# Cross attention with the probabilities turned on VectorE and placed by DMAs, sums two steps behind, text keys and values in a stage of their own

## The chip, the cores and the metric

The kernel runs on one core of one Trainium2 chip. The metric is the time of one execution on the device in microseconds (us), the median of several runs. The core has a matrix engine (TensorE; PE in the profile, PEld its weight loads), VectorE (DVE), ScalarE (ACT), GpSimd (POOL), a queue processor that issues DMAs (SP) and 16 DMA engines. The matrix engine writes to PSUM, 8 banks of 128 partitions by 2 KB; all else lies in SBUF, 128 partitions.

## What is computed

Six layers work on an array x of 16 batches, 64 tokens, 256 features, each adding its result to x: a local attention, a self attention and a mixture of experts, then the cross attention that is changed here, a state-space scan and a second mixture of experts. The cross attention has 16 heads of 64 features. A batch's 64 queries look at 1601 context rows, in two softmaxes: 77 text rows and 1524 image rows, each with keys and values from weights of its own.

```python
ctx_txt, ctx_img = context[:, :77], context[:, 77:]
q = (x @ Wq).reshape(B, N, 16, 64)
out    = attend(q, heads(ctx_txt @ Wk),    heads(ctx_txt @ Wv))     # softmax(q k^T / 8) v
out_ip = attend(q, heads(ctx_img @ Wk_ip), heads(ctx_img @ Wv_ip))
return (out + out_ip) @ Wo + bo
```

## The kernel before

Each layer is one or more stages; a stage ends when all engines have left it. The stages that matter here: `positions_stage` (where the local attention looks), `near_attention` (the local attention's common case), and `cross_attention`.

`cross_attention` keeps the raw context rows instead of image keys and values. For a batch and a pair of heads, `key_side` (L2145) multiplies the pair's 128 queries (2 heads by 64 tokens) by the key weights, giving `a` (128 queries by 256 features, turned). `scores` (L2159 to L2161) multiplies `a` by the context `ct` in three banks of 508 columns. To keep float32 exactness at the matrix engine's fast rate each operand is split into a rounded part (`hi`) and the rest (`lo`), so a product is three: hi by hi, hi by lo, lo by hi. 

A step is one batch and one pair of heads: 8 pairs by 2 batches are the 16 steps (`STEPS`) of a tile, and 8 tiles make 128 steps. In step n, in program order, TensorE does: the text scores (L2151) once the exponentials of step n-1 are there; the 12 transposes of step n-1's image probabilities (`turn`, L2169, blocks of 127 columns, to PSUM); scores of step n; the transpose of the text probabilities (`turn_text`, L2176); of the sums of step n-2 (`turn_sums`, L2190); `key_side` of step n+1; `sums` of step n-1 (L2182: `pt_hi` by `cn` hi and lo side by side, 512 columns; L2183: `pt_lo` by `cn` hi, 256 columns; 12 times each); `value_side` of step n-2 (L2201, L2203). In 8 steps of a tile it also makes a piece of the next text keys or values in float32 (`text_keys`, L2127, 3 pieces a tile; `text_values`, L2136, 4 pieces a tile), in one step the next tile's queries (L2117), and in one the output projection (L2213).

VectorE takes the row maxima of the scores in PSUM (L2417, L2418), makes the bias (L2421), the rest parts `a_lo` and `pt_lo` (L2308, reading the product's PSUM bank and the `hi` part), the reciprocals (L2408), scales the text probabilities (L2410) and adds the two halves of the sums (L2432, L2435). ScalarE copies `hi` parts out of PSUM (L2302), takes the exponentials with their sums (L2365 image, L2368 text) and makes the plain copies (L2332). The scores have one buffer (`s_ps`), so the text scores of step n+1 wait for `exp_done` of step n. The other products go round a ring of 3 banks (`Ring`, `t_ps`).

SP loads the context of the next batch in 8 pieces (L1900 `ct`, L2032 `cn`), one staging buffer for all; GpSimd splits each piece into hi (L1907) and lo (L1909), after which SP may load the next. In `near_attention` SP first issues 32 small DMAs that bring the positions back from device memory (`load_positions`, L303), for which GpSimd's L603 waits.

Of the kernel before, what the change touches and what calls it, by code (L numbers as in the profile page):

```python
# [20 lines left out]
BANK = 512  # L21
# [32 lines left out]
IB, IBLK = 12, 127  # L54
SB, SBLK = 3, 508
assert IB * IBLK == IMG and SB * SBLK == IMG
# [392 lines left out]

def near_attention(nc, k, src, ctx):  # L450
# [299 lines left out]
def far_attention(nc, k, src):  # L750
# [3 lines left out]
    with ExitStack() as ctx:  # L754
# [39 lines left out]
        def _(sp):  # L794
            load_positions(sp, k)
# [1071 lines left out]
class Ring:  # L1867

    def __init__(self, i, uses_per_tile, splits_per_tile, at, splits):
        assert uses_per_tile % RING == 0
        self.i, self.each, self.split_each, self.at, self.splits = i, uses_per_tile // RING, splits_per_tile, at, splits

    def place(self, back=0):

        at = self.at - back
        return at % RING, self.i * self.each + (at // RING + 1)

    def next(self, split=False):
        got = self.place()
        self.at += 1
        self.splits += 1 if split else 0
        return got

    def split_count(self):
        return self.i * self.split_each + self.splits

# [27 lines left out]
class CrossFirst:  # L1918
# [3 lines left out]
    def __init__(self, nc, scope, src):  # L1922
        def sb(name, shape, dt=F32):
# [6 lines left out]
        self.wk_txt = sb("wk1_txt", [P, C, INNER])  # L1930
        self.text = sb("text1", [P, C, 2, TXT])
        self.staged = sb("staged", [P, CNB * D])
        self.ct = sb("ct0", [P, 2, C, IMG], F32R)
        self.wq_in, self.wk_in, self.text_in, self.piece_in, self.hi_done, self.ct_split, self.split_begun = (
            scope.enter_context(nc.semaphore(n))
            for n in ("wq1_in", "wk1_in", "text1_in", "piece_in", "ctx_hi_done", "ct_split", "ctx_split_begun"))

    def load_weights(self, sp):
        sp.dma_start(self.wq, self.src["wq1"]).then_inc(self.wq_in, 16)
        sp.dma_start(self.wk_txt[:], self.src["wk1_txt"]).then_inc(self.wk_in, 16)  # L1940
        sp.dma_start(self.text[:], self.src["ctx_txt"][0]).then_inc(self.text_in, 16)
# [3 lines left out]
def cross_attention(nc, k, src, first):  # L1945

    STEPS = 2 * PAIRS1
    K_USES, V_USES = 3, 2
    USES = STEPS * 7 + 4 + K_USES + 2 * V_USES  # L1950
    SPLITS = STEPS * 4
    SCALE = HD1 ** -0.5
    with ExitStack() as ctx:
# [9 lines left out]
        staged, wk, wk_txt, text, wq = first.staged, first.wk, first.wk_txt, first.text, first.wq  # L1963
        wo = first.w_shared[:].rearrange("p (h d) -> p h d", h=PAIRS1)
        wv = sb("wv1", [P, 2, C, INNER])
# [7 lines left out]
        prob = sb("prob1", [P, M])  # L1973
        pt_hi, pt_lo = sb("pt_hi", [P, IB, P], F32R), sb("pt_lo", [P, IB, P], F32R)
        pt_txt = [sb(f"pt_txt{s}", [P, P]) for s in range(2)]
        top = [sb(f"top1{s}", [P, 2]) for s in range(2)]
        bias = [sb(f"bias1{s}", [P, 2]) for s in range(2)]
        total = [sb(f"total1{s}", [P, 2]) for s in range(2)]
        inv = [sb(f"inv1{s}", [P, 2]) for s in range(2)]
        o, o_part = sb("o1", [P, D]), sb("o1_part", [P, D])  # L1980
# [6 lines left out]
        text_in, text_used = first.text_in, sem("text1_used")  # L1987
        queried, projected, bo_added = sem("queried"), sem("projected"), sem("bo1_added")
        piece_in, hi_done, ct_split, cn_split = first.piece_in, first.hi_done, first.ct_split, sem("cn_split")
        scored, topped, bias_done, exp_done = sem("scored1"), sem("topped1"), sem("bias1_done"), sem("exp1_done")  # L1990
        t_done = [sem(f"t1_done{j}") for j in range(RING)]
        t_kept = [sem(f"t1_kept{j}") for j in range(RING)]
        hi_kept, txt_normed = sem("hi_kept"), sem("txt_normed")
        summed, inv_done, part_kept, sums_kept = sem("summed1"), sem("inv1_done"), sem("part1_kept"), sem("sums1_kept")
        q_zeroed = sem("q_zeroed")
        block = ctx.enter_context(nc.Block())

        def tiles(eng, body):

            start = 2 + K_USES + 1  # L2000
            body(0, Ring(0, USES, SPLITS, start, 1), True, False)
# [970 lines left out]
```

## Time and profile before

| | us |
|---|---|
| median of 3 runs | 2601.33 (2599.84 to 2604.13) |
| the profiled execution | 2598.55 |
| its span, first to last instruction | 2595.7 |
| cross attention on TensorE, 551.3 to 2168.4 | 1617.1 |

The profile describes one execution. Its page gives busy times by engine and groups of instructions; behind it stand the timeline (instructions in order of time, runs of the same merged, with the idle time ahead and what ended it), the waits (who waited for whom) and stretches (busy time within given bounds, with the clock granted to TensorE, 1.00 being full). A matmul's duration in a timeline runs to a modelled end and overlaps the next, so what one costs is the distance between starts. The page's slices show the granted clock of TensorE at nine tenths or more through the cross attention.

### The profile page before, as it was taken

What the parts mean: (1) busy time and instruction counts of PE and PEld (TensorE: products, weight loads), DVE (VectorE), ACT (ScalarE), POOL (GpSimd) and SP (SyncE); (2) the same over time, 40 slices, a digit from 0 to 9 for tenths busy, and PEclk for the clock granted to TensorE, in tenths of its full rate; (3) what the DMA queues carried; (4) which work ended last, traced back from release to release, by engine and by line L of the source; (5) the groups of instructions that cost most, each with busy time, mean ns of one, the idle gap of its engine ahead of it and who ended that gap; (6) DMA issues with size and microseconds to landing.
All of it is one profiled execution on the core that took longest, in us unless ns stands there. A gap on an engine that the chain in (4) does not pass through costs nothing. (4 is left out here: it accounts for less than half of the span.)

```text
span 2595.7 us, 35955 instructions
## 1 busy us (share of the span) xinstructions
PE 2336.1 (90%) x13845; PEld 1831.3 (71%) x13845; DVE 1311.2 (51%) x2478; ACT 957.0 (37%) x2031; POOL 858.2 (33%) x534
## 2 busy tenths in 40 slices
PE   3787759949999999999999999999999997788896
PEld 2454446647888888888888888888888884334683
DVE  3897533334544544544544544544444444785553
ACT  1564121123443443433443443443443443442330
POOL 2663225225413414314314214224223100352444
PEclk8899869979999999999999999999999998787898
DMA  3100063122102112102102002102101005001372
GB/s 101 16 13 6 1 231 112 35 96 58 43 29 62 37 34 63 37 29 68 31 17 86 25 19 84 31 19 63 46 25 60 7 1 211 0 0 41 102 147 89
DMA packets 69927, 141.32 MB, mean 54 GB/s; under 512 B 24912, under 2 KB 42576, under 8 KB 65408
## 3 DMA queue, kind: packets, MB, share of 16 engines
q1 hardware_dynamic: 62992, 120.50, 14.7%
q0 software_dynamic: 6768, 18.49, 3.1%
q8 instruction: 117, 1.92, 0.3%
q14 instruction: 50, 0.41, 0.1%
HBM read 124.21 MB, written 14.75 MB: 54 GB/s over the span
## 5 line engine op out<-in xcount | busy, mean ns | idle before, releaser
L2182 PE MATMUL img_ps<-cn,pt_hi 127*128 127x512 f32 x1536 | 551.4, 400 | 6.7 <-POOL cn L1909 6.6
L2183 PE MATMUL img_ps<-cn,pt_lo 127*128 127x256 f32 x1536 | 430.0, 280 | 0.0
L1907 POOL TENSOR_SCALAR ct<-staged 128x762 fp32r<-128x762 f32 x64 | 136.2, 2128 | 756.5 <-DMA staged<-in_ctx_t 527.2
L2182 PEld LDWEIGHTS img_ps<-cn,pt_hi 127*128 127x128 f32 x1536 | 289.7, 189 | 66.5 <-POOL cn L1909 6.8
L2308 DVE TENSOR_TENSOR pt_lo<-t_ps,pt_hi 127x512 fp32r<-127x512 f32 x384 | 241.4, 684 | 141.1 <-ACT pt_hi L2302 141.1
L2159 PE MATMUL s_ps<-ct,a_hi 128*128 128x508 f32 x768 | 312.3, 407 | 0.0
L2161 PE MATMUL s_ps<-ct,a_lo 128*128 128x508 f32 x768 | 301.6, 393 | 0.0
L2160 PE MATMUL s_ps<-ct,a_hi 128*128 128x508 f32 x768 | 301.5, 393 | 0.0
L2183 PEld LDWEIGHTS img_ps<-cn,pt_lo 127*128 127x128 f32 x1536 | 289.6, 189 | 0.0
L2365 ACT ACTIVATE prob<-s_ps,bias 128x1524 f32<-128x1524 f32 x128 | 196.7, 1536 | 143.0 <-DVE bias L2421 143.0
L2302 ACT ACTIVATE pt_hi<-t_ps 127x512 fp32r<-127x512 f32 x384 | 202.1, 599 | 80.8 <-PE t_ps L2169 77.0
L2418 DVE TENSOR_REDUCE top<-s_ps 128x1 f32<-128x1524 f32 x128 | 222.1, 1735 | 0.0
L2432 DVE TENSOR_SCALAR o_part<-img_ps,inv 128x256 f32<-128x256 f32 x128 | 61.9, 483 | 301.4 <-PE img_ps L2183 301.4
L1907 POOL TENSOR_SCALAR cn<-staged 128x768 fp32r<-128x768 f32 x64 | 136.7, 2136 | 228.8 <-DMA staged<-in_ctx_n 182.0
L2332 ACT ACTIVATE pt_txt<-t_ps 77x128 f32<-77x128 f32 x128 | 35.0, 273 | 453.5 <-PE t_ps L2176 453.5
L2169 PE MATMUL t_ps<-small,prob 128*127 128x128 f32 x1536 | 196.9, 278 | 0.0
L2417 DVE TENSOR_REDUCE top<-s_ps 128x1 f32<-128x77 f32 x128 | 30.5, 238 | 321.1 <-PE s_ps L2161 321.1
L2169 PEld LDWEIGHTS t_ps<-small,prob 128*127 128x127 f32 x1536 | 180.7, 191 | 0.1
L2161 PEld LDWEIGHTS s_ps<-ct,a_lo 128*128 128x128 f32 x768 | 144.7, 188 | 31.9
L2160 PEld LDWEIGHTS s_ps<-ct,a_hi 128*128 128x128 f32 x768 | 145.6, 190 | 27.4
L2159 PEld LDWEIGHTS s_ps<-ct,a_hi 128*128 128x128 f32 x768 | 144.9, 189 | 27.2
L1632 PE MATMUL up_ps_b<-up_all_m,xt_b 128*128 x436 | 152.2, 481 | 2.1 <-ACT xt_b L1678 0.9
(369 smaller groups left out, 3944.8 us busy)
## 6 DMA issues: line engine op xcount, KB each, us to landing
staged<-in_ctx_n SPq DMA_DIRECT2D x64, 384.0 KB, 3.1
staged<-in_ctx_t SPq DMA_DIRECT2D x64, 381.0 KB, 3.2
up_all_m<-in_up SPq DMA_DIRECT2D x8, 2048.0 KB, 13.1
down_all_m<-in_down SPq DMA_DIRECT2D x8, 1024.0 KB, 23.0
sums_m<-y_b SPq DMA_DIRECT2D x63, 128.0 KB
w_shared<-in_wq SPq DMA_DIRECT2D x7, 1024.0 KB, 5.7
w_shared<-in_wo SPq DMA_DIRECT2D x7, 1024.0 KB, 4.9
win<-in_ctx_near SPq DMA_DIRECT2D x16, 128.0 KB, 2.0
```

What stands on the lines that cost most here:

```text
L1632: last = nc.tensor.matmul(up_ps[j % 2][:, own], xt[j % 2][:, c, :], m.up[:, bass.ds(expert, 1), c, own].rearrange("p a h -> p (a h)"), sta ...
L1907: nc.gpsimd.tensor_scalar(hi, piece, 1.0, None, ALU.mult).then_inc(first.hi_done, 1)
L2159: nc.tensor.matmul(out, a_hi[:, c, :], ct[b][:, 0, c, cols], start=c == 0, stop=False)
L2160: nc.tensor.matmul(out, a_hi[:, c, :], ct[b][:, 1, c, cols], start=False, stop=False)
L2161: last = nc.tensor.matmul(out, a_lo[:, c, :], ct[b][:, 0, c, cols], start=False, stop=c == C - 1)
L2169: last = nc.tensor.transpose(t_ps[bank][0:IBLK, j * P:(j + 1) * P], prob[:, at:at + IBLK], k.ident)
L2182: nc.tensor.matmul(img_ps[:], pt_hi[0:IBLK, j, :], rows[0:IBLK, :, j, :], start=j == 0, stop=False)
L2183: last = nc.tensor.matmul(img_ps[:, D:2 * D], pt_lo[0:IBLK, j, :], rows[0:IBLK, 0, j, :], start=False, stop=j == IB - 1)
L2302: nc.scalar.activation(out, t_ps[bank][0:rows, 0:cols], ACT.Copy).then_inc(hi_kept, 1)
L2308: nc.vector.tensor_tensor(out, t_ps[bank][0:rows, 0:cols], hi.bitcast(F32), ALU.subtract).then_inc(t_kept[bank], 1)
L2365: nc.scalar.activation(prob[:, TXT:M].rearrange("p (j m) -> p j m", j=SB), s_ps[:, 1:4, 0:SBLK], ACT.Exp, bias=bias[s][:, 1:2], scale=SCAL ...
L2418: nc.vector.tensor_reduce(top[s][:, 1:2], s_ps[:, 1:4, 0:SBLK], mybir.AxisListType.XY, ALU.max).then_inc(topped, 1)
```

## The change

1. **Turning.** The 12 transposes on TensorE go. The image probabilities get 12 columns of zeros (`prob` is now 77 + 12 by 128 wide, `ctx_n` is laid out in blocks of 128 rows). VectorE turns them with 4 transposes per step, each 128 partitions by 384 elements and each element within its own 32 by 32 block, into `blocks`. 16 DMAs per step (32 partitions by 384 elements, 48 KB each) put the blocks in their place in `moved` (two buffers). ScalarE copies `moved` to `pt_hi` in two halves (128 by 768 elements), VectorE makes `pt_lo` of the same halves.
2. **Sums two steps behind.** `sums` of step g-2 stand in step g (g-1 before), in two halves, each matmul 256 columns and all three products of a block added up in one half bank; so VectorE has one scaling (no `o_part`). `value_side` is three steps behind.
3. **Text stage.** `text_stage`, between `positions_stage` and the local attention, makes the text keys and values of all 16 batches and writes them to device memory (`k_txt`, `v_txt`); the cross attention loads them by DMAs. Its weights are loaded with the first stage's. `load_positions` moves from the near attention to the head of this stage's SP program.
4. The loop over tiles is written out with plain counters.

The diff, cut to its core:

```diff
+def text_stage(nc, k, w):
+    BANKS = 8
+    K_COLS = [slice(0, 3 * 2 * TXT), slice(3 * 2 * TXT, 6 * 2 * TXT), slice(6 * 2 * TXT, TEXT)]
+    uses = [("k", p, cols) for p in range(PAIRS1) for cols in K_COLS]
+    uses += [("v", t, slice(h * BANK, (h + 1) * BANK)) for t in range(V_TILES) for h in range(2)]
...
+        def _(sp):
+            load_positions(sp, k)
+            for p in range(PAIRS1):
+                wait_kept(sp, len(K_COLS) * (p + 1))
+                sp.dma_start(k.k_txt[:, :, p, :].rearrange("i q n -> q i n"),
+                             keys[p % 2][:].rearrange("q (i n) -> q i n", i=NT)).then_inc(keys_out[p % 2], 16)
...
+        def _(pe):
+            pe.wait_ge(w.keys_in, 32)
+            for u, (kind, at, cols) in enumerate(uses):
+                if u >= BANKS:
+                    pe.wait_ge(kept[u % 2], (u - BANKS) // 2 + 1)
...
+        def keep(eng, copy, mine):
+                eng.wait_ge(done, u + 1)
+                if at >= 2:
+                    eng.wait_ge((keys_out if kind == "k" else values_out)[at % 2], 16 * (at // 2))
...
 near_attention, @block.sync
-        load_positions(sp, k)
...
 cross_attention, @block.sync
+            for g in range(N):
+                s, (i, b, p, n) = g % 2, parts(g)
+                for m in range(Q):
+                    sp.wait_ge(turned, Q * g + m + 1)
+                    if m == 0 and g >= 2:
+                        sp.wait_ge(split_done, 2 * (g - 1))
+                    for a in range(Q):
+                        sp.dma_start(moved[s][m * QR:(m + 1) * QR, a], blocks[a * QR:(a + 1) * QR, m]).then_inc(moved_in[s], 16)
+                if g // PAIRS1 + 1 < NB:
+                    load(g // PAIRS1 + 1, g % PAIRS1)
...
 @block.tensor
-            def turn(ring, g):
-                bank = use(ring, True)
-                for j in range(4):
-                    last = nc.tensor.transpose(t_ps[bank][0:IBLK, j * P:(j + 1) * P], prob[:, at:at + IBLK], k.ident)
...
+            def sums(g):
+                if g:
+                    pe.wait_ge(sums_kept, g)
+                for h in range(2):
+                    pe.wait_ge(split_done, 2 * g + h + 1)
+                    for j in range(IB)[half(h)]:
+                        for at, (left, right) in enumerate(((pt_hi, 0), (pt_hi, 1), (pt_lo, 0))):
+                            last = nc.tensor.matmul(img_ps[:, 0:D], left[0:n, j, :], rows[0:n, right, j, :],
+                                                    start=j == 0 and at == 0, stop=j == IB - 1 and at == 2)
+                    last.then_inc(summed if h else half_summed, 1)
...
+            for g in range(N + 3):
+                if g < N:
+                    if g:
+                        pe.wait_ge(exp_done, g)
+                    kept(a_place)
+                    text_scores(g)
+                    scores(g)
...
 @block.scalar
+                if 1 <= g <= N:
+                    act.wait_ge(moved_in[(g - 1) % 2], 16 * Q * Q * ((g - 1) // 2 + 1))
+                    for h in range(2):
+                        if g >= 2:
+                            act.wait_ge(summed if h else half_summed, g - 1)
+                        nc.scalar.activation(in_quarters(pt_hi, h), by_block(moved[(g - 1) % 2], h),
+                                             ACT.Copy).then_inc(pt_hi_kept, 1)
...
 @block.vector
+                    dve.wait_ge(image_exp, g + 1)
+                    if g:
+                        dve.wait_ge(moved_in[(g - 1) % 2], 16 * Q * Q * ((g - 1) // 2 + 1))
+                    source = prob[:, TXT:].rearrange("p (j m c) -> p m j c", j=IB, m=Q)
+                    for m in range(Q):
+                        nc.vector.transpose(blocks[:, m], source[:, m]).then_inc(turned, 1)
...
+                if 1 <= g <= N:
+                    for h in range(2):
+                        dve.wait_ge(pt_hi_kept, 2 * (g - 1) + h + 1)
+                        nc.vector.tensor_tensor(in_quarters(pt_lo, h), by_block(moved[(g - 1) % 2], h),
+                                                in_quarters(pt_hi, h).bitcast(F32), ALU.subtract).then_inc(split_done, 1)
+                if 2 <= g <= N + 1:
+                    dve.wait_ge(summed, g - 1)
+                    nc.vector.tensor_scalar(o[:], img_ps[:, 0:D], inv[(g - 2) % 3][:, 1:2], None,
+                                            ALU.mult).then_inc(sums_kept, 1)
```

The order on three engines, in the middle of the cross attention. TensorE before, from the end of one step's sums to the next step's scores, in a step with a piece of text values:

```order
L2182 MATMUL img_ps<-cn,pt_hi 128x512
L2183 MATMUL img_ps<-cn,pt_lo 128x256
L2201 MATMUL t_ps<-ot,wv 64x64 x4
L2203 MATMUL t_ps<-pt_txt,v_txt 64x64 x2
L2136 MATMUL t_ps<-wv,text 77x512 x2
L2151 MATMUL s_ps<-k_txt,q 128x77
L2169 MATMUL t_ps<-small,prob 127x128 x12
L2159 MATMUL s_ps<-ct,a_hi 128x508
```

TensorE after, from the scores' end to the first sums (L2245 `turn_text`, L2267 `turn_sums`, L2216 `key_side`, L2259 `sums`):

```order
L2238 MATMUL s_ps<-ct,a_lo 128x508
L2245 MATMUL t_ps<-small,prob 77x128
L2267 MATMUL t_ps<-small,o 128x128 x2
L2216 MATMUL t_ps<-q,wk 128x128 x2
L2259 MATMUL img_ps<-cn,pt_hi 128x256 x2
L2259 MATMUL img_ps<-cn,pt_lo 128x256
```

The transposes L2169 and the text pieces are gone, and the sums are 36 matmuls of 256 columns. VectorE before, one step from the reciprocal on:

```order
L2408 RECIPROCAL inv<-total 128x2
L2410 TENSOR_SCALAR prob<-prob,inv 128x77
L2308 TENSOR_TENSOR pt_lo<-t_ps,pt_hi 127x512 x3
L2417 TENSOR_REDUCE top<-s_ps 128x1
L2418 TENSOR_REDUCE top<-s_ps 128x1
L2421 TENSOR_SCALAR bias<-top 128x2
L2308 TENSOR_TENSOR a_lo<-t_ps,a_hi 128x256
L2432 TENSOR_SCALAR o_part<-img_ps,inv 128x256
L2435 SCALAR_TENSOR_TENSOR o<-img_ps,inv,o_part 128x256
```

VectorE after, one step from the maxima on (`pairs` holds maxima, biases, totals and reciprocals):

```order
L2437 TENSOR_REDUCE pairs<-s_ps 128x1
L2438 TENSOR_REDUCE pairs<-s_ps 128x1
L2441 TENSOR_SCALAR pairs<-pairs 128x2
L2425 TENSOR_TENSOR a_lo<-t_ps,a_hi 128x256
L2454 STREAM_TRANSPOSE prob_blocks<-prob 128x384 x4
L2456 RECIPROCAL pairs<-pairs 128x2
L2458 TENSOR_SCALAR prob<-prob,pairs 128x77
L2466 TENSOR_TENSOR pt_lo<-prob_moved,pt_hi 128x768 x2
L2470 TENSOR_SCALAR o<-img_ps,pairs 128x256
```

Between the bias and the reciprocal of a step now stand its four transposes; the `pt_lo` behind them belong to the step before. The SP queue before, over 4 batches' loads:

```order
L1900 DMA staged<-in_ctx_t 128x762 x4
L2032 DMA staged<-in_ctx_n 128x768 x4
L2053 DMA w_shared<-in_wo 128x2048
L1900 DMA staged<-in_ctx_t 128x762 x4
L2032 DMA staged<-in_ctx_n 128x768 x4
```

The SP queue after, two steps and more:

```order
L2122 DMA k_txt<-k_txt_rows 128x616
L2141 DMA prob_moved<-prob_blocks 32x384 x16
L2117 DMA staged<-in_ctx_n 128x768
L2125 DMA v_txt<-v_txt_rows 77x1024
L2141 DMA prob_moved<-prob_blocks 32x384 x16
```

Each step's 16 moves now stand between one piece of the context and the next.

## Rows read from the trace of the kernel before

**Rows 1.** Stretches: length, busy us by engine (PE first), granted clock, DMA share, GB/s.

```profile
40.00:50.00 10.00, 0.19 (x2) 0.09 (x2) 7.78 (x13) 0.00 (x0) 1.67 (x2) 0.50 0.16 42
551.30:2168.40 1617.10, 1602.47 (x10496) 1364.84 (x10496) 762.82 (x1440) 645.51 (x1481) 487.10 (x249) 1.00 0.14 41
```

**Rows 2.** What TensorE waited for, 560 to 2080 us: us, times, longest.

```profile
PE img_ps L2182 <- POOL cn L1909: 6.6, 1, 6.6
...
PE s_ps L2151 <- ACT prob L2368: 2.0, 1, 2.0
```

**Rows 3.** Timeline of TensorE, a step: start us, us, line, operation.

```profile
2131.72 0.45 PE L2151 MATMUL s_ps<-k_txt,q 128*128 128x77 f32 x2
2132.01 1.53 PE L2169 MATMUL t_ps<-small,prob 128*127 128x128 f32 x12
2133.30 0.48 PE L2159 MATMUL s_ps<-ct,a_hi 128*128 128x508 f32 x1
...
2138.52 0.28 PE L2183 MATMUL img_ps<-cn,pt_lo 127*128 127x256 f32 x1
2138.64 0.39 PE L2182 MATMUL img_ps<-cn,pt_hi 127*128 127x512 f32 x1
...
2143.04 0.45 PE L2151 MATMUL s_ps<-k_txt,q 128*128 128x77 f32 x2
```

**Rows 4.** Timeline of TensorE: text keys of a tile; two starts of steps.

```profile
557.26 4.37 PE L2127 MATMUL t_ps<-text,wk_txt 128*128 128x154 f32 x32
...
1006.72 0.34 PE L2151 MATMUL s_ps<-k_txt,q 128*128 128x77 f32 x2
...
1019.73 0.34 PE L2151 MATMUL s_ps<-k_txt,q 128*128 128x77 f32 x2
```

**Rows 5.** Timeline of VectorE in the step of rows 3.

```profile
2132.44 0.26 DVE L2410 TENSOR_SCALAR prob<-prob,inv 128x77 f32<-128x77 f32 x1
2133.32 1.89 DVE L2308 TENSOR_TENSOR pt_lo<-t_ps,pt_hi 127x512 fp32r<-127x512 f32 x3 [0.61 <-ACT pt_hi L2302]
2137.71 0.24 DVE L2417 TENSOR_REDUCE top<-s_ps 128x1 f32<-128x77 f32 x1 [2.51 <-PE s_ps L2161]
...
2139.72 0.42 DVE L2308 TENSOR_TENSOR a_lo<-t_ps,a_hi 128x256 fp32r<-128x256 f32 x1
2142.65 0.48 DVE L2432 TENSOR_SCALAR o_part<-img_ps,inv 128x256 f32<-128x256 f32 x1 [2.52 <-PE img_ps L2183]
```

**Rows 6.** Timeline of ScalarE in the same step.

```profile
2139.84 1.53 ACT L2365 ACTIVATE prob<-s_ps,bias 128x1524 f32<-128x1524 f32 x1 [0.97 <-DVE bias L2421]
...
2141.57 0.20 ACT L2368 ACTIVATION_READ_ACCUMULATOR prob<-s_ps,bias 128x1 f32 x1
```

**Rows 7.** Timeline, 1204.9 to 1212.3 us: a normalisation beside GpSimd's splits.

```profile
1204.93 1.81 POOL L1909 TENSOR_TENSOR cn<-staged,cn 128x768 fp32r<-128x768 f32 x1
...
1205.44 1.35 DVE L2410 TENSOR_SCALAR prob<-prob,inv 128x77 f32<-128x77 f32 x1
...
1210.14 2.13 POOL L1907 TENSOR_SCALAR cn<-staged 128x768 fp32r<-128x768 f32 x1 [3.41 <-DMA staged<-in_ctx_n]
```

**Rows 8.** Timeline of the SP queue: DMAs issued back to back.

```profile
11.31 0.43 SPq L2819 DMA_DIRECT2D biases<-in_biases  x1
11.78 0.43 SPq L2819 DMA_DIRECT2D o_w<-in_wo  x1
...
49.49 1.81 SPq L303 DMA_DIRECT2D pos<-pos_rows  x5
...
55.74 5.02 SPq L303 DMA_DIRECT2D pos<-pos_rows  x4
```

**Rows 9.** Issue to landing of lines L2032 (384 KB) and L507 (128 KB).

```profile
DMA to landing us min/median/max: 3.0/3.1/8.5
...
DMA to landing us min/median/max: 1.9/2.0/4.1
```

**Rows 10.** GpSimd's waits, 48 to 90 us, for the positions' loads.

```profile
POOL tent L603 <- DMA pos<-pos_rows: 13.9, 2, 7.5
```

More of the change, by code:

```diff
@@ L2089, in _, with use @@
                                     ALU.add).then_inc(bo_added, 1)
-            for i in range(1, NT):
-                for b in range(2):
-                    split(i, b)
+            for b in range(2, NB):
+                split(b)
         @block.tensor
         def _(pe):
-            def use(ring, split=False):
-                bank, count = ring.next(split)
-                if not isinstance(count, int) or count > 1:
+            ring = Ring()
+            def use():
+                bank, count = ring.next()
+                if count > 1:
@@ L2147, in key_side, with text_scores @@
                 last.then_inc(t_done[bank], 1)
-            def text_scores(n):
-                b, p = divmod(n, PAIRS1)
+                return ring.place(1)
+            def text_scores(g):
+                i, b, p, n = parts(g)
+                if n in (0, 4):
+                    pe.wait_ge(k_in, 32 * i + (16 if n and i else 32 if not i else 16) + (16 if n and i else 0))
                 nc.tensor.matmul(s_ps[:, 0, 0:TXT], q[:, p, b].rearrange("p r n -> p (r n)"), k_txt[:, p, b, :],
                                  start=True, stop=True)
-            def scores(n, g):
-                b = n // PAIRS1
-                cols = slice(g * SBLK, (g + 1) * SBLK)
-                out = s_ps[:, 1 + g, 0:SBLK]
-                for c in range(C):
-                    nc.tensor.matmul(out, a_hi[:, c, :], ct[b][:, 0, c, cols], start=c == 0, stop=False)
-                    nc.tensor.matmul(out, a_hi[:, c, :], ct[b][:, 1, c, cols], start=False, stop=False)
-                    last = nc.tensor.matmul(out, a_lo[:, c, :], ct[b][:, 0, c, cols], start=False, stop=c == C - 1)
-                return last
@@ L2178, in sums, with scores @@
-            def sums(n):
-                rows = cn[n // PAIRS1]
-                for j in range(IB):
-                    nc.tensor.matmul(img_ps[:], pt_hi[0:IBLK, j, :], rows[0:IBLK, :, j, :], start=j == 0, stop=False)
-                    last = nc.tensor.matmul(img_ps[:, D:2 * D], pt_lo[0:IBLK, j, :], rows[0:IBLK, 0, j, :],
-                                            start=False, stop=j == IB - 1)
-                last.then_inc(summed, 1)
-            def turn_sums(ring):
-                bank = use(ring)
+            def scores(g):
+                b = g // PAIRS1 % 2
+                if g % PAIRS1 == 0:
+                    pe.wait_ge(ct_split, 4 * (g // PAIRS1) + 4)
+                for t in range(SB):
+                    cols = slice(t * SBLK, (t + 1) * SBLK)
+                    out = s_ps[:, 1 + t, 0:SBLK]
+                    for c in range(C):
+                        nc.tensor.matmul(out, a_hi[:, c, :], ct[b][:, 0, c, cols], start=c == 0, stop=False)
+                        nc.tensor.matmul(out, a_hi[:, c, :], ct[b][:, 1, c, cols], start=False, stop=False)
+                        last = nc.tensor.matmul(out, a_lo[:, c, :], ct[b][:, 0, c, cols], start=False, stop=c == C - 1)
+                last.then_inc(scored, 1)
```

631 lines of the change are left out of this document (304 added, 327 removed).

## The prediction, made before the changed kernel ran

> **What bounds the kernel now.** I read the stretches first. Over the cross attention, 1617 us of the span, TensorE is busy for 1602 at a granted clock of 1.00 [rows 1]; the waits view puts its idle time there at 6.6 us for the first context pieces and 2.0 us for one exponential [rows 2]. So this stage is TensorE's own work, and whatever leaves TensorE shortens it until another ring of dependences becomes the longest. A step without extras takes 2143.04 - 2131.72 = 11.32 us, and a step with a piece of text values 1019.73 - 1006.72 = 13.01 [rows 3, 4].
>
> **What leaves TensorE.** The 12 transposes stand from 2132.01 to 2133.30 [rows 3]: 1.29 us a step, 128 steps, 165 us. The sums keep their cost: before, a 512-column matmul and a 256-column one per block, and the 256-column one starts 0.12 us ahead of the next [rows 3]; three of 256 columns at 0.12 each are the same 0.35 us or so a block, 12 blocks. Should the extra weight loads not hide beneath 0.12 us the bound is a few hundredths a block; I take none, since a load already hides there. The text values cost 13.01 - 11.32 = 1.69 us a piece, 32 pieces, 54 us; the text keys 4.37 us a tile [rows 4], 8 tiles, 35 us. Together 254 us off TensorE's path in this stage, and a plain step becomes 10.03 us.
>
> At the edges: the sums now need a move before them, so behind the last scores stand the exponential, the transposes, 16 DMAs and their landing, the split and the sums. From the start of the last step, 2143.04 [rows 3], to the end of the stage at 2168.4 it took 25 us; by the terms below I count about 31. The beginning still waits for the first four pieces of `cn`, behind five loads instead of one. I put both at +6 us, bounds 0 and +15. The cross attention: 254 - 6 = 248 us less, as long as TensorE stays the bound.
>
> **What the text stage costs.** Nothing of this stage runs beside it but the positions' loads, so it stands in the span whole. Values: 10 tiles of rows by 2 halves at 1.69 us, 34 us (before 32 pieces, as 77 rows filled a piece badly). Keys: the same columns, 35 us. TensorE comes to it cold: the clock was 0.50 in the 10 us before [rows 1]; estimate, 3 us. SP must first issue the 32 position DMAs, 16 at 1.81/5 = 0.36 us and 16 at 5.02/4 = 1.25 us [rows 8], some 25 us. TensorE can fill two key buffers and 8 banks meanwhile, 14 of 24 key products, 20 + 3 us; the first store, issued at 25 and landing like a 384 KB load in 3 to 4 us [rows 9], frees it at 29. Stall 6 us. The end, last copy, store and leaving, about 4. Sum 34 + 35 + 3 + 6 + 4 = 82 us, bounds 73 and 105 (stores slower, cold clock again after the stall). In return the near attention finds its positions there: GpSimd waited for them 13.9 us in two waits [rows 10]; I credit 12, bounds 6 and 14. Net +70.
>
> **Can the rest keep a step of 10.03 us?** I set VectorE's first maximum of a step at 0 (2137.71 in [rows 5]). The image exponential starts at 2.13 and, with its accumulator, ends near 3.75; the text one ends at 4.06 (2141.57 + 0.20) [rows 6]. TensorE wants it at 2143.04, 5.33: slack 1.3 us, unchanged by the change.
>
> VectorE. A transpose of 128 by 384 has no row. Nearest: subtraction of 256 elements 0.42 us, three of 512 in 1.89, so 0.63 each in a row, 1.0 ns an element [rows 5]. At that rate a transpose takes 0.50 in a row; from below half of that, from above twice, 0.90. I take 0.50, the rate of the row nearest to it. VectorE then goes: exponential ready 3.75, four transposes 5.75, reciprocal and normalisation 6.2, two halves of `pt_lo` at 0.90 (768 elements) 8.0, one scaling of 0.48 where two stood [rows 5], 8.5. Slack 1.5 us. ScalarE has two copies of 768 elements in place of three of 512 and stays near 5 us of work.
>
> GpSimd beside VectorE. In [rows 7] a normalisation that takes 0.26 us when GpSimd rests [rows 5] took 1.35 and ended at 1206.79, when GpSimd's subtraction ended (1206.74). It cost nothing, TensorE being the bound. Now a piece of context is split in every step (2.13 + 1.81 us of GpSimd), at a phase fixed by the SP queue, and the new `pt_lo` has both inputs in SBUF, where the old one read PSUM. No row shows such an operation beside GpSimd: its wait lies between nothing and one GpSimd subtraction, 1.8 us, a step. Walking the phase: first transpose done at 4.3, 16 issues, the load of the next piece, landing 3.1 us later [rows 9], split begins at 13.6 to 15.3, that is 3.5 to 5.3 in the next step, and ends at 7.6 to 9.4; the normalisation is due at 6.0 and the two `pt_lo` behind it. If only the normalisation waits, VectorE ends at 10.0 to 10.1 and the step stays 10.03 to 10.1; if a `pt_lo` also lets one subtraction by, the step becomes (15.3 + 2.15 + 0.25 + 1.84 + 1.8 + 0.5)/2 = 10.9. I take the middle, 10.4: +0.37 us a step, 128 steps, +47 us.
>
> The Trainium skill bears on this (SBUF — State Buffer, Who interferes with whom): a VectorE instruction with two SBUF inputs and a GpSimd one that reads SBUF shut each other out for a whole instruction. For the normalisation the trace agrees, 1.35 us against 0.26; for two SBUF inputs no run here shows it. By the page the step is the 10.9 more often than the 10.1.
>
> The SP queue. VectorE may not begin the transposes of step g+1 before the moves of step g have landed. That ring is: first transpose 0.55, SP's start 0.1, 15 issues, four waits of 0.05, issue to landing of the last, VectorE's start 0.1. Issues in a row cost 0.36 us (small, 8 partitions) or 0.47 (11.31 to 11.78, 128 partitions) [rows 8]; a 128 KB transfer lands in 2.0 us, 1.9 at least [rows 9]. So 15 x 0.36 gives 8.4 us, 15 x 0.47 gives 10.0: just inside a step. The loads of pieces are issued while the last moves land and cost the ring nothing; a piece's own cycle, 3.1 landing and 4.0 split, is shorter than a step. What these 16 queue behind at tile ends is a 1 MB weight load; the moves have 3 us of slack against ScalarE there, so I count nothing.
>
> **The sum.** 2598.55 - 248 + 70 + 47 = 2468 us against the profiled execution; the median stands 2.8 us above that, so 2470.
>
> **Rivals.**
> *TensorE stays the bound* (10.03 to 10.15 a step): no +47, so 2423. For it: VectorE ends at 8.5 without waits and GpSimd may lose the race instead. Against it: three rings within 0.3 us of one another and one GpSimd split a step.
> *Transposes at half rate*: 0.90 instead of 0.50 adds 1.6 to VectorE's 8.5 and 0.4 to the SP ring; with some of the GpSimd waits about 11.0 a step, 2423 + 0.97 x 128 = 2547. For it: a strided source in runs of 32 elements; against it: the maxima, which have one input as well, take about 1.1 ns an element (the 1524 of a step lie within 2137.71 and 2139.72, the start of `a_lo` [rows 5]).
> *The SP queue is the bound, and the kernel slower.* The gain is used up at 10.03 + (248 - 70)/128 = 11.42 us a step. The SP ring reaches that when issues cost 0.56 us each: 0.55 + 0.1 + 15 x 0.56 + 0.2 + 2.0 + 0.1. At 0.60 it is 11.95, and the kernel takes 2423 + 1.92 x 128 = 2669. For it: in [rows 8] the queue slowed to 1.25 us an issue once it had enough small descriptors before it, and landings reach 4.1 and 8.5 us [rows 9]. Against it: those had 112 rows of 20 bytes per partition, these have one row of 1536 bytes.
>
> The Trainium skill's rule for small transfers (DMA: Bandwidth & Descriptors, Rules for kernel authors) is that below 64 KB a transfer is mostly overhead; these are 48 KB. That speaks for this rival; the sum above prices the overhead by rows.
>
> **How the numbers follow.** Forecast (10.15 to 10.8 a step, 2440 to 2520) 0.44; TensorE bound, 2423, 0.24; half-rate transposes or the like, 10.8 to 11.4, to 2600, 0.12; SP bound past 11.42, 0.20, nearly all of it slower. With the text stage's bounds the lowest sum is 2410. The range 2410 to 2600 leaves out the last case. A measurement of this kernel tells 0.2%, 5 us, from no change: faster 0.78, same 0.02, slower 0.20.
>
> **What would show it.** Right: steps of about 10.4 us; TensorE's idle time, now nil, at `s_ps` (text scores) behind ScalarE's exponential, which is late since VectorE began its maxima late; `pt_lo` and the normalisation longer than 0.9 and 0.26 when a split runs; issues of the moves at 0.36 to 0.47; a text stage near 82 us. Wrong: VectorE's transposes waiting for a DMA landing in most steps (then the SP ring is the bound); transposes of 0.8 us or more; the granted clock below 1.00 in the cross attention, which would raise every term; a text stage past 105 us.

## The result: 6.8% slower

| | before | after |
|---|---|---|
| median of the runs on one chip, us | 2602.73 (2599.84 to 2605.01) | 2780.61 (2773.49 to 2786.25) |
| span of the profiled execution, us | 2595.7 | 2780.6 |
| cross attention on TensorE, us | 1617.1 | 1720.7 (632.3 to 2353.0) |
| its start | 551.3 | 632.3 |

The ratio is 1.068, 95% interval 1.0654 to 1.0705, over four runs of each. The forecast was 2470, the range 2410 to 2600. The span grew by 184.9 us: cross attention begins 81.0 later (forecast 70) and takes 103.6 longer (forecast 201 shorter: 248 less the 47 for the steps of 10.4).

First the stretch of the cross attention, answering [rows 1] (busy us by engine, PE first, then clock, DMA share, GB/s). TensorE has less to do and idles 256 us, and the clock is no longer whole:

```profile
632.00:2353.00 1721.00, 1464.81 (x10112) 1302.85 (x10112) 960.17 (x1696) 605.27 (x1297) 536.24 (x250) 0.94 0.39 102
```

The waits of all engines in that stage, those behind the moves and then TensorE's own (us, times, longest), where [rows 2] had 6.6 and 2.0:

```profile
DVE prob_blocks L2454 <- DMA prob_moved<-prob_blocks: 583.1, 112, 14.8
...
ACT pt_hi L2402 <- DMA prob_moved<-prob_blocks: 384.9, 110, 13.1
...
PE t_ps L2267 <- DVE o L2470: 161.7, 92, 4.8
...
PE t_ps L2245 <- DVE prob L2458: 26.0, 23, 9.3
PE t_ps L2295 <- ACT head_out L2367: 25.6, 7, 4.5
```

In 112 of 128 steps VectorE's first transpose (L2454) waits for the sixteen moves of the step before. What TensorE waits for (`o`, the text probabilities) stands behind those transposes in VectorE's order. The ring shows in the timelines of SP's queue and of VectorE over one step:

```profile
1300.15 10.35 SPq L2141 DMA_DIRECT2D prob_moved<-prob_blocks  x16
1310.55 1.49 SPq L1990 DMA_DIRECT2D staged<-in_ctx_t  x1
1313.66 3.67 SPq L2141 DMA_DIRECT2D prob_moved<-prob_blocks  x6
```

```profile
1299.55 1.96 DVE L2454 STREAM_TRANSPOSE prob_blocks<-prob 128x384 f32<-128x384 f32 x4 [4.13 <-DMA prob_moved<-prob_blocks]
...
1301.59 0.91 DVE L2458 TENSOR_SCALAR prob<-prob,pairs 128x77 f32<-128x77 f32 x1
1302.42 1.81 DVE L2466 TENSOR_TENSOR pt_lo<-prob_moved,pt_hi 128x768 fp32r<-128x768 f32 x2
1304.16 0.47 DVE L2470 TENSOR_SCALAR o<-img_ps,pairs 128x256 f32<-128x256 f32 x1
...
1313.05 1.96 DVE L2454 STREAM_TRANSPOSE prob_blocks<-prob 128x384 f32<-128x384 f32 x4 [6.10 <-DMA prob_moved<-prob_blocks]
```

The first issue starts 0.60 us in, the sixteen take 10.35, the last move lands 2.45 us after its issue has ended, and 0.1 later, at 1313.05, 13.50 behind 1299.55, the next transposes start. VectorE stood idle 6.10 us of it. This round is a long one: its last move landed 3.0 us after the start of its issue, where the median is 1.9. An undisturbed round is 0.61 + 10.01 + 1.32 + 0.09 = 12.03 us. Over all moves (issue duration in ns, min/median/max, and landing):

```profile
L2141 SPq DMA_DIRECT2D prob_moved<-prob_blocks x2048: 507/591/2148, 662.5 to 2334.4; - x187
...
DMA to landing us min/median/max: 1.8/1.9/5.5
```

With about 0.05 us between issues a move costs the queue 0.64 us, where I had 0.36 to 0.47 [rows 8]. Put in my own ring that is 0.55 + 0.1 + 15 x 0.64 + 0.2 + 1.9 + 0.1 = 12.5 us; the 0.2 for four waits is not in the trace. The starts of the text scores, step to step, have a median of 12.06 us and a mean of 13.15 (127 intervals); before, 11.33 and 12.44. The mean is lifted by two steps of each tile: step 2 (output projection) takes 21 to 23 us, step 15 (next tile's queries) 19 to 23.

### The profile page after: what moved, and what is told of

Read it like the earlier page. It is cut to its first block and busy times, and to the rows that moved or that the text cites. A ratio compares the mean times of both kernels' runs of the same rounds, so it can differ in the third digit from the quotient of the medians.

```text
span 2780.6 us, 38344 instructions
## 1 busy us (share of the span) xinstructions
PE 2271.1 (82%) x13637; PEld 1804.2 (65%) x13637; DVE 1521.8 (55%) x2756; ACT 928.2 (33%) x1869; POOL 907.1 (33%) x535
## 5 line engine op out<-in xcount | busy, mean ns | idle before, releaser
L2259 PE MATMUL img_ps<-cn,pt_hi 128*128 128x256 f32 (+1 forms) x3072 | 606.1, 299 | 0.0
L2454 DVE STREAM_TRANSPOSE prob_blocks<-prob 128x384 f32<-128x384 f32 x512 | 250.5, 546 | 605.2 <-DMA prob_moved<-prob_blocks 583.1
L2259 PEld LDWEIGHTS img_ps<-cn,pt_hi 128*128 128x128 f32 (+1 forms) x3072 | 509.3, 203 | 0.0
L2259 PE MATMUL img_ps<-cn,pt_lo 128*128 128x256 f32 (+1 forms) x1536 | 450.9, 294 | 0.0
L2402 ACT ACTIVATE pt_hi<-prob_moved 128x768 fp32r<-128x768 f32 x256 | 204.3, 839 | 401.4 <-DMA prob_moved<-prob_blocks 384.9
L2259 PEld LDWEIGHTS img_ps<-cn,pt_lo 128*128 128x128 f32 (+1 forms) x1536 | 310.2, 202 | 0.0
L2466 DVE TENSOR_TENSOR pt_lo<-prob_moved,pt_hi 128x768 fp32r<-128x768 f32 x256 | 285.9, 1157 | 9.5 <-ACT pt_hi L2402 9.3
L2390 ACT ACTIVATE prob<-s_ps,pairs 128x1524 f32<-128x1524 f32 x128 | 196.5, 1535 | 103.8 <-DVE pairs L2441 103.7
L2438 DVE TENSOR_REDUCE pairs<-s_ps 128x1 f32<-128x1524 f32 x128 | 221.6, 1731 | 0.0
L2267 PE MATMUL t_ps<-small,o 128*128 128x128 f32 x256 | 55.3, 300 | 162.1 <-DVE o L2470 161.9
L2267 PEld LDWEIGHTS t_ps<-small,o 128*128 128x128 f32 x256 | 28.6, 148 | 189.5 <-issue 186.7
L1999 POOL TENSOR_TENSOR cn<-staged,cn 128x768 fp32r<-128x768 f32 x64 | 123.0, 1922 | 5.3
```

The lines of the kernel that those rows point to most:

```text
L1999: nc.gpsimd.tensor_tensor(lo, piece, hi.bitcast(F32), ALU.subtract).then_inc(done, 1)
L2259: last = nc.tensor.matmul(img_ps[:, 0:D], left[0:n, j, :], rows[0:n, right, j, :], start=j == 0 and at == 0, stop=j == IB - 1 and at == 2)
L2390: nc.scalar.activation(prob[:, TXT:M].rearrange("p (j m) -> p j m", j=SB), s_ps[:, 1:4, 0:SBLK], ACT.Exp, bias=bias[g % 2][:, 1:2], scale= ...
L2402: nc.scalar.activation(in_quarters(pt_hi, h), by_block(moved[(g - 1) % 2], h), ACT.Copy).then_inc(pt_hi_kept, 1)
L2438: nc.vector.tensor_reduce(top[g % 2][:, 1:2], s_ps[:, 1:4, 0:SBLK], mybir.AxisListType.XY, ALU.max).then_inc(topped, 1)
L2454: nc.vector.transpose(blocks[:, m], source[:, m]).then_inc(turned, 1)
```

## Experiments

Each is compared by its ratio to the kernel before, run on the same chip beside it: 2590.1 us beside the first four (waits by quarters, twelve moves, half bytes, quarter on ScalarE), 2603 to 2605 beside the rest. Diffs are against the changed kernel unless another is named.

**1. One wait or four.** Do the issues pace the step, or does the single wait for all sixteen?

```diff
-                    if g:
-                        dve.wait_ge(moved_in[(g - 1) % 2], 16 * Q * Q * ((g - 1) // 2 + 1))
                     for m in range(Q):
+                        if g:
+                            dve.wait_ge(moved_in[(g - 1) % 2][m], 16 * Q * ((g - 1) // 2 + 1))
                         nc.vector.transpose(blocks[:, m], source[:, m]).then_inc(turned, 1)
```

> VectorE waits before each of its four transposes only for the four moves that read the same quarter in the step before, not for all sixteen; nothing else changes. Theory (the ring of issue and landing is the bound): 16 issues at 0.64 us and a landing of 1.9 us no longer add up, what stays is the SP queue's own pace, 16 x 0.64 + one piece load of 0.63 = 10.9 us a step, so about 2781 - 128 x 1.4 = 2600 us, and nearly no wait of VectorE for moves. Rival (the moves are late because the DMA engines are slow at them): the wait stays, 2750 or more. Rival (GpSimd's splits hold VectorE up): no change either, 2780.

Measured 2638.73 us, ratio 1.018 (1.0158 to 1.0209), where 2600 were expected; the long steps at the ends of a tile stayed at 21.5 and 20.3 us. The steps have a median of 11.17 us and a mean of 12.20, so the plain ones now stand near SP's own work of a step, 16 x 0.64 + 0.6 for the piece's load = 10.9 us. The wait for the last landing was 5% of the kernel; against TensorE's 10.1 (below) the issues still hold back the plain steps.

**2. Twelve moves, and half the bytes.** Is it their number or their size? Both kernels leave out a part of the placing and write zeros there once.

```diff
-                    for a in range(Q):
+                    for a in range(Q - 1):
                         sp.dma_start(moved[s][m * QR:(m + 1) * QR, a], blocks[a * QR:(a + 1) * QR, m])
```

> Leaves out 4 of the 16 moves of each step (the last block row; that part of moved is set to zero once), all waits as in the changed kernel. Theory: the ring shortens by 4 x 0.64 = 2.6 us a step until TensorE's 10.0 to 10.4 us is the bound: 2500 to 2540 us. Rival (GpSimd's splits hold VectorE up): 2750 or more.

> All 16 moves, each of half the bytes (32 rows of 768 bytes; the other half of moved is set to zero once). If an issue costs SP a fixed 0.59 us, the issues stay at 0.59, only the landing gets 0.1 to 0.2 us shorter and the time stays within 2750 to 2781. If the cost comes from the bytes that the DMA engines move, issues fall to 0.45 or less and the time below 2650.

Twelve moves: 2479.19 us, ratio 0.957 (0.9545 to 0.959), median step 10.12, below the 2500 to 2540 expected. Sixteen of half size: 2746.35, ratio 1.060 (1.0573 to 1.0624), the issue as long as with whole ones:

```profile
L2141 SPq DMA_DIRECT2D prob_moved<-prob_blocks x2048: 507/590/1893, 661.0 to 2313.5; - x187
```

So a move's price on the queue is per issue. This decides for the third rival, the SP queue as the bound.

**3. A second queue.** Two versions give ScalarE's queue the last quarter's four moves, with waits by quarters and with the one wait:

```diff
-                for m in range(Q):
+                for m in range(Q - 1):
                     sp.wait_ge(turned, Q * g + m + 1)
...
+                if g < N:
+                    act.wait_ge(turned, Q * g + Q)
+                    if g >= 2:
+                        act.wait_ge(split_done, 2 * (g - 1))
+                    for m in range(Q - 1, Q):
+                        for a in range(Q):
+                            nc.scalar.dma_start(moved[g % 2][m * QR:(m + 1) * QR, a], ...)
```

> e1 and besides, the four moves of the last quarter are issued by ScalarE behind its copies instead of by SP. Theory: SP's pace falls to 12 x 0.64 + 0.63 = 8.3 us, ScalarE gets 2.6 us more work on 7, and TensorE (10.03) or VectorE beside GpSimd (10.1 to 10.9) is the bound: 10.1 to 10.5 us a step, 2510 to 2560 us, faster than the kernel before. Rival (both queues share what makes an issue cost 0.59): issues get dearer on both, 2600 or more.

> The changed kernel with one edit: ScalarE's queue issues the four transfers of the last quarter, SP's the other twelve; VectorE still waits for all sixteen before its first transpose. My theory, that SP's issues (0.59 us each, 0.64 apart) set the step: twelve take 7.6 us, the last lands 1.9 later, so the ring is 0.6 + 7.6 + 1.9 = 10.1 us, TensorE's own 10.03 us decides, and what is left is the long steps at the tile ends: 2510 to 2540 us, ratio about 0.975. Rival, that it is the joint wait that costs (the wait by quarters alone gave 142 us): the sixteen still land as one block, step near 12, 2640 us or more. Second rival, that the transfers themselves share a limit however they are issued: no gain, 2780 us.

By quarters 2513.56 us, ratio 0.970 (0.9682 to 0.9726); with the one wait 2532.24, ratio 0.971 (0.9683 to 0.9745). Median steps 10.11 and 10.12. Once no queue has more than twelve issues, the form of the wait does not matter, and the kernel is faster than before. The Trainium skill (DMA: Bandwidth & Descriptors, Issuing engines are not separate DMA queues) says that issuing from several engines saves only the sequencer's time to initiate, "which is usually small relative to the DMA itself". Here that time was the bound.

**4. The long steps at the ends of a tile.** With the plain steps at 10.1 us, step 2 still took 20.2 us and step 15 16.8. The timeline of step 2 with ScalarE's four issues, TensorE and ScalarE, and the stretches around it (columns as above):

```profile
1034.80 1.58 ACT L2403 ACTIVATE pt_hi<-prob_moved 128x768 fp32r<-128x768 f32 x2 [1.51 <-DMA prob_moved<-prob_blocks]
...
1035.74 2.51 ACTq L2413 DMA_DIRECT2D prob_moved<-prob_blocks  x4
...
1038.30 0.22 ACT L2367 ACTIVATE head_out<-t_ps 128x64 f32<-128x64 f32 x1 [1.92 <-issue]
...
1038.58 6.76 PE L2295 MATMUL t_ps<-w_shared,head_out 128*128 128x128 f32 x32 [3.80 <-ACT head_out L2367]
```

```profile
1034.70:1038.50 3.80, 0.07 (x4) 0.00 (x0) 3.76 (x7) 1.78 (x3) 2.44 (x1) 0.92 0.61 172
1038.50:1042.00 3.50, 3.42 (x16) 3.43 (x17) 0.30 (x1) 0.02 (x1) 1.94 (x2) 0.50 0.38 90
1042.00:1045.00 3.00, 3.00 (x17) 3.00 (x17) 0.29 (x1) 0.00 (x0) 0.00 (x0) 0.54 0.51 146
1045.00:1049.00 4.00, 4.00 (x21) 3.38 (x21) 0.29 (x1) 0.00 (x0) 3.60 (x2) 1.00 0.00 0
```

The projection needs `head_out`, whose copy stands on ScalarE behind `pt_hi`, and so behind the moves' landing; in this version it stands behind ScalarE's own four issues too, and these 2.51 us ended last. With twelve moves, all on SP, and the same order, step 2 has a median of 14.5 us.
```diff
                 if boundary(g):
                     keep_queries(act, copy, 0, ring)
+                    keep_a(g + 1)
+                if g >= N or projects(g) is not None:
+                    keep_head(g)
                 if 1 <= g <= N:
                     ...                                 # the split: waits for the moves
-                if boundary(g):
-                    keep_a(g + 1)
...
                 if boundary(g):
                     keep_queries(dve, copy, 1, ring)
                     dve.sem_inc(queried, 1)
+                    keep_a_lo(g + 1)
```

> The kernel with waits by quarters and ScalarE's four issues, with two edits at the tile ends: in the step of the projection ScalarE copies head_out before it splits and issues, and in the last step of a tile ScalarE and VectorE copy a_hi and a_lo before they split. In the trace without it TensorE waits there 3.9 us (projection) and 3.3 us (next tile's scores), and its granted clock falls to 0.50 in the wait and stays there for the 6.6 us of the projection, which at clock 1.00 take 3.6. I expect both waits gone and the clock up: 7 x (3.9 + 3.0) + 7 x 3.3 = 71 us less, 2440 us, ratio to before 0.943; steps of the projection from 20.2 to 13.7 us. Rival, that the projection waits for the 1 MB of wo and not for ScalarE: projection steps stay near 20, only 23 us less, 2490 us. Second rival: the late split makes the next step late by as much, no gain.

> The kernel with waits by quarters and all sixteen transfers on SP's queue, with the order edits at the tile ends alone (head_out copied ahead of the split in the step of the projection; a_hi and a_lo ahead of it in the last step of a tile). Without them it took 1.018 of before, with steps of 21.5 and 20.3 us at the tile ends. Theory, that those steps are long by the order of the work and not by SP's pace: both fall to about 15, 7 x 6.5 + 7 x 5.3 = 82 us less, ratio 0.986. Rival, that SP's sixteen issues set these steps too: less than 20 us gained, ratio 1.01.

With ScalarE's issues and this order: 2459.27 us, ratio 0.945 (0.9426 to 0.9482). Step 2 takes 14.19 us and step 15 14.22 in every tile but the first, the others 10.02 to 10.12. The order alone, all moves on SP: 2603.64 us, ratio 1.000 (0.9988 to 1.0016). That is 47 us less by the ratios, where 82 were expected. Step 2 fell from 21.5 to 14.2 us, as the theory had it; step 15 only from 20.3 to 18.5, as the rival had it. There VectorE's copy of the next queries `q` stands behind the transposes, which still wait for the moves, and TensorE waits for that copy (VectorE, then TensorE, of the order alone):

```profile
1214.54 0.58 DVE L2459 STREAM_TRANSPOSE prob_blocks<-prob 128x384 f32<-128x384 f32 x1 [2.28 <-DMA prob_moved<-prob_blocks]
...
1215.38 1.38 DVE L2423 COPY q<-t_ps 64x512 f32<-64x512 f32 x2
...
1216.86 0.68 PE L2216 MATMUL t_ps<-q,wk 128*128 128x128 f32 x4 [2.66 <-issue]
```

With both edits TensorE is the bound again, at a clock of 0.99 (the whole stage, and without its two ends):

```profile
632.90:2029.80 1396.90, 1365.60 (x10112) 1235.95 (x10112) 942.58 (x1697) 614.33 (x1297) 525.67 (x250) 0.99 0.47 126
644.00:2005.00 1361.00, 1338.95 (x9922) 1211.02 (x9921) 933.67 (x1684) 609.03 (x1284) 525.58 (x249) 0.99 0.48 127
```

**5. What an issue costs.** Back to back with its like a move (SBUF to SBUF) takes 0.591 us, and 0.507 when the queue was idle. The load of a context piece from DRAM takes 0.33 from an idle queue, 0.43 behind another transfer from DRAM (before, and on the way through DRAM) and 0.58 behind a move. To see what makes the difference, three kernels start from the reordered one: one places through DRAM (four stores and four loads a step), one copies 128 partitions straight and leaves out the placing, and one cuts the first store of the way through DRAM into four of 32 rows.

```diff
+                    sp.dma_start(spill[s][m], blocks[:, m].rearrange("p j c -> p (j c)"))        # through DRAM
+                    sp.dma_start(moved[s][m * QR:(m + 1) * QR].rearrange("r a j c -> r a (j c)"),
+                                 spill[s][m].rearrange("(a r) e -> r a e", a=Q))
...
+                    sp.dma_start(moved[s][:, m], blocks[:, m])                                   # 128 straight
...
+                    for a in range(Q if m == 0 else 1):                                          # narrow stores
+                        rows = slice(a * QR, (a + 1) * QR) if m == 0 else slice(0, P)
+                        sp.dma_start(spill[s][m, rows], blocks[rows, m].rearrange("p j c -> p (j c)"))
```

> The same kernel with the placing done through DRAM: each turned quarter is stored with one transfer of 128 rows by 1536 bytes and loaded, placed, with one of 512 rows; eight issues a step on SP in place of sixteen, none on ScalarE; VectorE waits for the stores, ScalarE for the loads. Theory of a fixed cost for each issue: SP is busy 8 x 0.6 + 0.6 = 5.4 us of a step, the last load lands 0.6 + 4 x 0.6 + 4 x 0.6 + 2.5 = 8 us after the first transpose, TensorE bounds at 10.03 us a step, 2440 us, ratio 0.943 as with the kernel before this. Rival, that an issue costs by its rows (32 rows 0.59 us, then 128 rows over 1.5 us): SP is busy 4 x 1.5 + 4 x 1.5 = 12 us, step 13 and more, 2800 us. Second rival, that DRAM costs more (stores and loads of 4 us each): the loads come 2 to 3 us late, 2600 us.

> A measurement of the issue alone: four transfers a step, each from the 128 partitions of prob_blocks straight to the same 128 partitions of prob_moved, in place of sixteen between sets of 32 partitions; the bytes are the same, and the placing across partitions is left out of the computation. So far a move (SBUF to SBUF, 32 rows of 1536 bytes) has its issue last 0.507 us alone and 0.591 behind another, while stores of 128 rows to DRAM and loads of 128 placed rows take 0.32 to 0.35 alone and 0.40 to 0.43 behind another. Theory one, that it is the pair SBUF to SBUF: 0.51 alone, 0.59 behind another. Theory two, that it is the 32 rows: 0.33 and 0.43. The time is TensorE's either way, 2440 to 2470 us.

> The counterpart: the way through DRAM, with the store of the first quarter cut into four of 32 rows each (1536 bytes a row, 48 KB), the others left at 128 rows. Theory one (SBUF to SBUF costs): the narrow stores issue in 0.35 alone and 0.43 behind another like the wide ones. Theory two (32 rows cost): 0.51 alone and 0.59 behind another. SP has 11 issues a step, at most 7 us, so the time stays at 2460 to 2480 us.

The lines of the straight copies, of the stores (7 a step, 4 of them narrow) and of the placing loads from DRAM, issue in ns, min/median/max:

```profile
L2140 SPq DMA_DIRECT2D prob_moved<-prob_blocks x512: 464/602/2077, 665.6 to 2001.9; - x171
```

```profile
L2145 SPq DMA_DIRECT2D prob_spill<-prob_blocks x896: 302/422/1930, 662.7 to 2004.5; - x180
```

```profile
L2148 SPq DMA_DIRECT2D prob_moved<-prob_spill x512: 302/328/1451, 664.8 to 2010.6; - x171
```

From an idle queue the straight copies take 0.465 us and behind one another 0.607, though they have 128 rows; the stores 0.313 and 0.423, though most have 32 (all medians). So it is the pair SBUF to SBUF that costs, not the rows. The way through DRAM took 2468.43 us, ratio 0.947 (0.9439 to 0.9499): eight issues a step on one queue, twice the transfers' bytes, and TensorE the bound all the same. The other two took 2456.82 and 2459.18, one run each.

**6. The positions.** The 32 loads back where they were, in the changed kernel and in the fastest:

```diff
 text_stage, first thing on SP
-            load_positions(sp, k)
 near attention, and the other blocks that use them
+            load_positions(sp, k)
```

> The changed kernel with one edit: the 32 loads of relative positions go back from the text stage to the near attention and the blocks that used them before. SP then issues 26 us less ahead of the text keys. I expect the text stage to end about 12 us earlier (TensorE's wait of 12.05 us for text_keys goes) and the near attention to take the 7 us back that it had gained: 5 us less in all, between 0 and 12, ratio to the changed kernel 0.998, and cross attention on TensorE unchanged at 1720 us. Rival, that the wait for text_keys hangs on the weight loads and not on the positions: the text stage keeps its length and the time rises by 7 us.

> The fastest kernel so far (ratio 0.945) with the positions loaded where they were before. On the changed kernel that took TensorE's 12.05 us wait for text_keys away and gave 9.3 us of waits in the near attention back; cross attention began 1.1 us earlier. I expect the same here: 1 to 4 us less, not to be told from no change, ratio 0.944. Rival: the whole 12 us show, ratio 0.941.

Measured 2776.2 us, ratio 1.067 (1.0626 to 1.0714), and 2452.03, ratio 0.942 (0.9398 to 0.9448). TensorE's 12.05 us wait for `text_keys` went in the first, as expected, and 9.3 us of waits in the near attention came back. The two versions can't be told from those with the positions in the text stage. The last one is the fastest measured, 5.8% under before.

## Why the forecast failed, step by step

**The step that failed** is the SP ring. "So 15 x 0.36 gives 8.4 us, 15 x 0.47 gives 10.0: just inside a step." The durations in [rows 8] are those of loads from DRAM; none was an SBUF to SBUF transfer, and those hold the queue 0.59 us each, 0.64 with the gap. My break-even for the whole kernel was 0.56 an issue, and at 0.60 I had 11.95 us a step and 2669 us. So the third rival, to which I gave 0.20, had the path, the condition and the direction right, and the sign that I had named for it, VectorE's transposes waiting for a landing in most steps, came in 112 of 128. Its reasons were not what happened, though: I had argued for it with an issue of 1.25 us and late landings, and against it with the shape of the rows. The moves take 0.59 us at the median and land in 1.9, and of what the runs varied, 24 to 192 KB and 32 or 128 partitions, nothing changed an issue by more than 0.05 us, while the pair SBUF to SBUF adds 0.16 to a DRAM transfer's 0.43. The Trainium skill's rule on transfers under 64 KB (DMA: Bandwidth & Descriptors, Rules for kernel authors) pointed the right way, though the straight copies of 192 KB held the queue as long. A cost table in the same page, for DMAs that GpSimd issues (Anatomy of one DMA — SWDGE (gpsimd) path), lays most of a transfer's fixed cost to the receipt and calls the making of descriptors "small, variable"; these moves went through SP's queue, their landing of 1.9 us was priced right, and the issue was what bound.

**A second step: "so I count nothing"** at the tile ends. It was not the 1 MB load that came late, but the copies for TensorE that stand behind the split, and the split waits for the moves. In the changed kernel step 2 takes 21.6 us in the mean and step 15 20.6, against 14.2 with both edits. There are seven of each with a projection or new queries, 7 x 7.4 + 7 x 6.4 = 97 us; step 2 of the first tile projects nothing, takes 19 us even with both edits, and adds 3. A price of 11.95 us for every step, as at 0.60 an issue, has 15 x 1.92 = 29 of these 100; the other 71 are most of what lies between that 2669 and the 2781 that came. The rest is the other steps, 112 at 12.07 in the mean (13 us), the end of the stage behind the start of the last step, 44 us where I had 31 (13), and the text stage (11).

**The clock.** "The granted clock below 1.00 in the cross attention" was named as a sign of a wrong forecast, with no price. It fell to 0.94 over the stage. TensorE's busy time there is 1464.81 us, against 1365.60 with as many matmuls at 0.99 in the whole stage of the reordered kernel. How much of these 99 us lies under waits that were there anyway was not measured apart; at the projection they reached the end.

**The text stage** came to +81.0 us at the start of the cross attention, forecast 70. The stall was 12.05 instead of 6:

```profile
81.47 15.63 PE L524 MATMUL text_ps<-text_all,wk_txt 128*128 128x308 f32 x40 [12.05 <-ACT text_keys L545]
```

```profile
47.81 25.93 SPq L304 DMA_DIRECT2D pos<-pos_rows  x32
73.85 25.39 SPq L504 DMA_DIRECT2D k_txt_rows<-text_keys  x8
```

The positions' issues took the 25.9 us that I had (some 25), so the first store of keys was issued at 73.85; what I mis-sized is what TensorE can do until then. So the near attention started 88 us later, where I had 82, and the cross attention 81: behind the text stage 7 us came back rather than 12. GpSimd had waited 13.9 for the positions [rows 10], but TensorE's wait for the first context loads, 7.1 us where it had been 3.5, took part of that place. Both are small, and both sides of moving the positions cancel, as experiment 6 shows.

**What was right.** *TensorE's part*: with SP relieved, plain steps take 10.02 to 10.12 us, forecast 10.03, so the transposes were worth their 1.29 us and the sums, now 36 matmuls 0.12 us apart, cost no more than before. Step 2 takes 14.19 where 14.1 would follow from the same terms. *VectorE's transpose*: four in 1.96 us, 0.49 each, forecast 0.50; the half-rate rival falls. *The landing*: 1.9, forecast 2.0. *The edge*: from the start of the last step to the end of the stage the reordered kernel takes 35 us, forecast 31, before 25; the changed one takes 44.

**The GpSimd term, +47 us, was wrong, and hidden behind the larger error.** The mutual delays are there: in the rounds shown above a normalisation takes 0.84 to 0.91 us instead of 0.26, and `pt_lo` has a mean of 1157 ns in the changed kernel and 1077 in the reordered one, where one that no split overlaps takes 0.95:

```profile
L2480 DVE TENSOR_TENSOR pt_lo<-prob_moved,pt_hi 128x768 fp32r<-128x768 f32 x252 | 261.2, 1077 | 3.1 <-ACT pt_hi L2412 3.1
L2467 DVE STREAM_TRANSPOSE prob_blocks<-prob 128x384 f32<-128x384 f32 x512 | 252.6, 548 | 193.9 <-ACT prob L2396 170.5 <-DMA prob_moved<-prob_blocks 22.8
```

But 2 x (1.08 - 0.95) + (0.40 - 0.26), about 0.4 us a step, goes into VectorE's slack, 1.5 us by my own count, and the step stays at 10.10. The rule of two SBUF inputs cited from the Trainium skill holds in kind, as the longer `pt_lo` shows; the time that it costs here is at most 0.07 us a median step, 9 us, not 47. The normalisation, by which I had said that the trace agrees, has one array as input and a number for each row, so it is not the case of that rule; `pt_lo` is. Had SP's term been right, the first rival (TensorE stays the bound, 2423) would have been nearest: the reordered kernel is at 2459.

The chain from after to the fastest, by ratios to before: 1.068; waits by quarters 1.018; order at the tile ends 1.000; four issues on ScalarE's queue 0.945; positions 0.942, the last not to be told from none.

## What to carry to other kernels

A queue is an engine: count its issues per step times the duration of one, and put the sum beside the step. The duration must come from an issue of the same kind, source and destination both, behind its like; if the trace has none, keep the upper bound open and weigh it against the point at which it decides. Where a new wait enters an engine's program, look at each copy that stands behind it in every kind of step, the rare ones too: a few copies moved ahead of it were worth 1.8%, and a quarter of the issues moved to an idle queue 5.5%.

## What the runs showed of the hardware that I had not expected

- An SBUF to SBUF transfer holds the issuing queue 0.46 to 0.51 us from idle and 0.59 to 0.62 behind another (medians), on SP as on ScalarE (0.514 and 0.618), for 24, 48 and 192 KB and for 32 and 128 partitions nearly alike. For the stores and loads of the way through DRAM it is 0.30 to 0.34 and 0.35 to 0.42. Not all DRAM transfers are so cheap to issue: the later half of the positions' loads took 0.7 to 1.8 us each, 1.25 in [rows 8].
- The extra is also paid by the one behind: the same load of a context piece takes 0.43 us behind a DRAM transfer and 0.58 behind a move. The Trainium skill (Perfetto Trace Analysis, DMA Instruction — HWDGE (DVE, Sync)) says that the duration shown holds a wait for the lock on the descriptor generator; that would fit, and no run here shows the lock itself.
- Through DRAM, a store of 192 KB and a load that places it land in 2.0 and 3.6 us (medians), and the pair was no slower for the kernel than sixteen direct moves on two queues.
- TensorE's granted clock fell to 0.50 near the end of a wait of 3.8 us and stayed there for 6.1 of the 6.8 us of the projection behind it, though TensorE was busy throughout.
- GpSimd's splits lengthen a VectorE subtraction with both inputs in SBUF and leave one with an input in PSUM alone. In the changed kernel 45 of the 256 `pt_lo` overlap no split and take 0.95 to 0.96 us; the 211 that do take up to 2.57, though half of them 0.95 as well. In the kernel before, `pt_lo` read PSUM and took 0.67 to 0.69 with a split beside it (115 of 384) and without.
